# Two slots of 512 edges in each of two graph stages fetched row by row from SyncE's queue, in a two-network GNN kernel

## The reference, cut to what matters

```python
h = jnp.maximum(_layernorm(x), 0.0)
# first network, layers 0 and 1
msg = relu(x[src] + edge_attr)            # a gather of 100,000 rows of 512 bytes
agg = segment_sum(msg, dst, 6250)
h = (x + agg) @ W1 + b1; h = relu(batchnorm(h)); h = relu(h @ W2 + b2)
# second network, layers 2 and 3
agg = segment_sum(x[src], dst, 6250)
h = relu(((1 + eps) * x + agg) @ wA.T + bA) @ wB.T + bB
```

## Time and profile before

| | |
|---|---|
| median of 3 runs | 2780.12 us |
| the profiled execution | 2776.51 us |
| its span, first to last instruction | 2774.5 us |
| POOL busy | 1948.0 us (70%) |
| PE busy | 1915.5 us (69%) |
| DVE busy | 1712.8 us (62%) |
| ACT busy | 744.9 us (27%) |
| granted TensorE clock, mean | 0.846 of full |

### The profile page before, as it was taken

How to read it: one execution, slowest core, us unless ns; L and a number is a source line. 1 busy time by engine, 2 the same in 40 slices (tenths; PEclk the granted TensorE clock), 3 DMA queues, 4 the chain that set the end, 5 groups by cost and what they waited for, 6 DMA issues and landing times.

```text
span 2774.5 us, 30336 instructions
## 1 busy us (share of the span) xinstructions
PE 1915.5 (69%) x9233; PEld 1265.2 (46%) x9233; DVE 1712.8 (62%) x2755; ACT 744.9 (27%) x1002; POOL 1948.0 (70%) x2060
## 2 busy tenths in 40 slices
PE   3566565656665672656565666665678999989999
PEld 2444444434444442434343444433444565545656
DVE  7887777777776754777677767777764212442223
ACT  4222222222223241333333333333362000220001
POOL 6777777777777727777777777777706777367773
PEclk8788787777778886888778888888778999999999
DMA  6344333343434332444444444544425665466653
GB/s 198 113 128 120 113 112 115 116 125 113 128 112 143 120 116 85 121 149 128 142 135 150 134 151 148 162 152 157 142 83 193 222 211 199 140 205 214 219 191 115
DMA packets 224861, 403.74 MB, mean 146 GB/s; under 512 B 41224, under 2 KB 129116, under 8 KB 224740
## 3 DMA queue, kind: packets, MB, share of 16 engines
q1 hardware_dynamic: 159204, 267.94, 28.0%
q0 software_dynamic: 65536, 134.35, 18.3%
HBM read 337.92 MB, written 64.21 MB: 145 GB/s over the span
## 4 chain that ended last, share of the span: by engine, by line
POOL 47%; PE 26%; issue 17%; DVE 6%; DMA 3%; DVEq 1%; ACT 1%; POOLq 0%; SPq 0%; ACTq 0%
POOL xg L566 47%; PE psA L1354 17%; PE psG L1369 4%; DMA xg<-node_table,src_all 3%; PE psG L1418 2%; PE psA L1426 1%; DVE cell_room L960 1%; DVE xp_room L968 1%; DVEq L907 1%; DVE acc L885 0%; PE psG L1333 0%; PE psG L1448 0%; DVE xp_room L949 0%; DVE hid L932 0%; DVE hid L1065 0%
## 5 line engine op out<-in xcount | busy, mean ns | idle before, releaser
L566 POOL DMA_INDIRECT xg<-node_table,src_all x1536 | 1450.9, 945 | 513.5 <-issue 462.0
L1333 PE MATMUL psG<-hid,xp_room 128*128 128x160 f32 x3072 | 611.3, 374 | 414.0 <-DVE hid L932 400.8
L1333 PEld LDWEIGHTS psG<-hid,xp_room 128*128 128x128 f32 x3072 | 591.4, 253 | 466.1 <-issue 453.7
L1317 PE MATMUL psA<-cell_room,xp_room 128*128 128x512 f16 (+1 forms) x2176 | 552.4, 406 | 335.9 <-ACT count_out L633 247.8
L960 DVE TENSOR_SCALAR cell_room<-psG,cell_all 128x980 f16<-128x980 int16 x1088 | 712.2, 712 | 0.0
L586 POOL DMA_INDIRECT xg<-node_table,idx x480 | 461.2, 961 | 256.6 <-issue 253.2
L641 ACT COPY psG<-xp_room 128x512 f32<-128x512 f32 x384 | 226.4, 590 | 1246.7 <-DVE xp_room L968 1228.9
L968 DVE TENSOR_TENSOR xp_room<-psG,xg 128x512 f32<-128x512 f32 x384 | 261.9, 682 | 403.4 <-DMA xg<-node_table,src_all 399.0
L1317 PEld LDWEIGHTS psA<-cell_room,xp_room 128*128 128x128 f16 x2176 | 215.2, 104 | 629.8 <-ACT count_out L633 281.3
L885 DVE TENSOR_TENSOR acc<-acc,product 128x40 f32 x192 | 39.0, 203 | 395.3 <-ACT product L693 371.7
L932 DVE SCALAR_TENSOR_TENSOR hid<-loc_all,round_off,psG 128x2560 f32<-128x2560 f32 x96 | 274.7, 2861 | 0.0
(11 more groups left out here) (145 smaller groups left out, 794.3 us busy)
## 6 DMA issues: line engine op xcount, KB each, us to landing
xp_room<-in_edge_attr_dram SPq DMA_DIRECT2D x98, 768.0 KB, 4.8
cell_room<-count_store SPq DMA_DIRECT2D x16, 3000.0 KB
count_store<-count_out SPq DMA_DIRECT2D x96, 490.0 KB, 3.2
hid<-count_store SPq DMA_DIRECT2D x16, 2880.0 KB
xp_room<-in_edge_attr_dram SPq DMA_DIRECT2D x98, 256.0 KB, 5.1
xg<-node_table,src_all POOLq DMA_INDIRECT x1536, 2.5
node_table<-rows_h SPq DMA_DIRECT2D x48, 256.0 KB, 2.3
xg<-node_table,idx POOLq DMA_INDIRECT x480
```

The lines of the kernel that those rows point to most:

```text
L566: nc.gpsimd.indirect_dma_start(xg[:, n % 2, u, j, :], None, x if n < RAW_TURNS else table, bass.IndirectOffsetOnAxis(ap=src_all[:, s, j:j ...
L1317: last = nc.tensor.matmul(psA[:, bank, 0:w], src_hot[:, hots(n) % 2, i, :], cells[:, c % CELL_RING, c0:c0 + w], start=(c == first), stop=( ...
L1333: last = nc.tensor.matmul(psG[:, q, h * WIN:(h + 1) * WIN], ea[:, t, u, j, :], rows[:, u, j, :], start=(u == slots[0] and j == 0), stop=(u ...
```

## The change

In each of layers 0 and 1, slot 2 of turns 25 and 48 is no longer gathered by GpSimd. SyncE fetches its 512 rows with 512 DMAs of one row each. The address comes from a register: for each partition one load brings its four source numbers from `src_all` into registers, and four DMAs follow. They are handed out over the turns before: six partitions (24 DMAs) in each of turns 2 to 22 and two partitions in turn 23 for the slot of turn 25, and likewise in turns 26 to 46 and 47 for the slot of turn 48. They stand at the end of SP's turn, behind the attribute load. The rows go to a buffer of their own, `row_slot`, and `slot_sum` reads it for these slots.

```diff
+ROW_SLOT = 2
+ROW_TURNS = (25, TURNS - 1)
+ROW_STARTS = (2, 26)
+ROW_STEP = 6
...
+def by_rows(n, u):
+
+    return u == ROW_SLOT and n % TURNS in ROW_TURNS
+
+
+def landed(n, u):
+
+    return sum(not by_rows(t, u) for t in range(n % 2, n + 1, 2))
...
-        product = sb("product", [P, UPG, CW])
+        row_slot = sb("row_slot", [P, EPP * D])
+        product = row_slot[:, 0:UPG * CW].rearrange("p (s c) -> p s c", s=UPG)
...
+            def gather_rows(layer, t):
+
+                for k, (first, used) in enumerate(zip(ROW_STARTS, ROW_TURNS)):
+                    p0 = (t - first) * ROW_STEP
+                    if not 0 <= p0 < P:
+                        continue
+                    if t == first:
+                        sp.wait_ge(table_written, 16 * GROUPS * (layer + 1))
+                        if layer or k:
+                            last = (layer * TURNS + ROW_TURNS[k - 1] - (0 if k else TURNS)) * SLOTS + ROW_SLOT
+                            sp.wait_ge(summed, last + 1)
+                    s = used * SLOTS + ROW_SLOT
+                    for p in range(p0, min(p0 + ROW_STEP, P)):
+                        _, rows = nc.values_load_multi_w_load_instructions(
+                            src_all[p:p + 1, s, :], [mybir.EngineType.SP], min_val=0, max_val=NODES - 1,
+                            skip_runtime_bounds_check_because="the load checks its address against the table itself")
+                        for j, row in enumerate(rows):
+                            sp.dma_start(row_slot[p:p + 1, j * D:(j + 1) * D],
+                                         table[bass.DynSlice(row, 1), :]).then_inc(row_landed[k], 16)
...
                         load_turn(n + RING)
+                    gather_rows(layer, n % TURNS)
...
                     for u in range(SLOTS):
+                        if by_rows(n, u):
+                            continue
                         h = u // len(HALVES[0])
-                        if n >= 2 and u == HALVES[h][0]:
+                        if n >= 2 and u == min(v for v in HALVES[h] if not by_rows(n, v)):
...
                 dve.wait_ge(ea_staged, (n - RAW_TURNS) * SLOTS + u + 1)
-                dve.wait_ge(gathered[n % 2][u], 16 * EPP * (n // 2 + 1))
+                rows = xg[:, n % 2, u, :, :].rearrange("p j d -> p (j d)")
+                if by_rows(n, u):
+                    k, rows = ROW_TURNS.index(n % TURNS), row_slot[:, :]
+                    dve.wait_ge(row_landed[k], 16 * SUP * (n // TURNS + 1))
+                else:
+                    dve.wait_ge(gathered[n % 2][u], 16 * EPP * landed(n, u))
```

More of the change, by code:

```diff
@@ L345, in gnn_kernel @@
         gathered = [[sem(f"gathered{q}_{u}") for u in range(SLOTS)] for q in range(2)]
+        row_landed = [sem(f"row_landed{k}") for k in range(len(ROW_TURNS))]
         ea_staged = sem("ea_staged")
@@ L966, in slot_sum @@
                 dve.wait_ge(ea_staged, (n - RAW_TURNS) * SLOTS + u + 1)
-                dve.wait_ge(gathered[n % 2][u], 16 * EPP * (n // 2 + 1))
-                nc.vector.tensor_tensor(ea[:, n % RING, u, :, :].rearrange("p j d -> p (j d)"), ea_stage,
-                                        xg[:, n % 2, u, :, :].rearrange("p j d -> p (j d)"),
+                rows = xg[:, n % 2, u, :, :].rearrange("p j d -> p (j d)")
[4 more added lines that the diff above has]
+                    dve.wait_ge(gathered[n % 2][u], 16 * EPP * landed(n, u))
+                nc.vector.tensor_tensor(ea[:, n % RING, u, :, :].rearrange("p j d -> p (j d)"), ea_stage, rows,
                                         ALU.add).then_inc(summed, 1)
```

## The result

The changed kernel takes 2763.04 us in the median of four runs (2761.65 to 2765.65), the kernel before 2780.26 on the same chip (2774.67 to 2781.86, four runs). The ratio is 0.9942, with an interval of 0.9929 to 0.9954: faster, by 13 to 20 us. 2768 was forecast, and 2762 to 2773 as its own range. The profiled executions, 2761.72 and 2776.51 us, are 14.8 us apart, and the trace accounts for this difference. The gain of 11.6 us was given against the same execution. By the medians the gain is 17.2 us where 12 was forecast, so the result lies near the low end of the range.

The account below looks back on a forecast made before the run. GpSimd's issue of gathers was taken as the bound; 1.6 us from layer 0 and 10.0 from layer 1 sum to 11.6, about 12, giving 2768 us against the median. The range was 2757 to 2786, the forecast's own 2762 to 2773.

Parts of the forecast that it names:

- The bound: GpSimd's gathers in layers 0 and 1 set the pace, 1.249 us each; one not issued is worth 1.25 us.
- the new wait at the end of layer 0: DVE before slot 2 of turn 48: waits 7 us or more for rows issued in turn 47.
- the full gain of layer 1: End of layer 1: rows in time by some 0.6 us, so all 10.0 us are gained.
- SyncE's room in a turn: SyncE's steady turn: needs 16.4 to 16.7 us of 20, so it is in time every turn.
- one row DMA: Row fetch on SyncE: each DMA's issue takes 0.43 us, range 0.34 to 0.54.
- load of four registers: Row fetch on SyncE: one load per partition takes 0.8 us, range 0.3 to 1.28.
- gain of layer 0, at that sum: Slot 3's sum at layer 0's end: 996.6 instead of 998.24, a gain of 1.6 us, not 10.
- The landing of the last rows: End of layer 0: last two partitions issued until 992.8, landing taken as 2.5 us, so there at 995.3.
- Rival 3: Both layers: the full 20 us is gained, 2760, needing layer 0's last rows at 988; chance 0.06.
- Rival 2: Late stores delay ACT's evictions; layer 0's gain and part of layer 1's lost, 2773 to 2780; chance 0.17 with rival 4.
- Rival 4: 2048 small DMAs slow GpSimd's gathers, costing at most what the step gives; chance 0.17 together with rival 2.
- rival 1: SyncE becomes the bound above 3.1 us a partition: slower, about 2855 at 3.4 us; chance 0.17.

Follow-up runs that it names:

- the kernel one turn earlier: Against the changed kernel, turn 48's slot is fetched in turns 25 to 46, not 26 to 47: 2757.19 us, ratio 0.9908 to the kernel before.

## Why the prediction was right, and where it was not

The bound was right: each gather not issued gave 1.25 us (gathers still 1.249 us apart; the last of layer 0 issued 10.41 us earlier, of which 0.5 was there before turn 25). So were the new wait at the end of layer 0, the full gain of layer 1 with a gather as the last thing to arrive, and SyncE's room in a turn. By its steps:

| step | predicted | measured |
|---|---|---|
| one row DMA | 0.43 (0.34 to 0.54) | 0.228; 0.41 to 0.48 from one row's start to the next's, with two register instructions |
| load of four registers | 0.8 (0.3 to 1.28) | 0.562 in the median; 0.68 as 2.33 - 4 x 0.412 |
| one partition | 2.5 (1.7 to 3.4) | 2.33 |
| SyncE's turn, with attributes and one store | 16.4 | 15.3 |
| wait before slot 2 of turn 48, layer 0 | 7 to 11 | 7.76 |
| sum of slot 3, layer 0 | 996.6 | 993.92 |
| gain of layer 0, at that sum | 1.6 | 4.32 |
| gain of layer 1, at its last sum | 10.0 | 9.99 |
| last products of layer 1 | nothing | 1.94 |
| behind layer 1 | nothing | -1.46 |
| sum | 11.6 | 14.8 |

The one term of the sum that was mis-sized is layer 0's end, by 2.7 us, and it has two parts. The landing of the last rows was put at 2.5 us from the rows for stores and gathers; it is 1.14 us from the end of the last issue (991.43) to the sum (992.57), and 1.68 at the end of layer 1 (2003.74 to 2005.42). That is 1.36. The other 1.2 is the start: turn 47's products were over, and SyncE free, at 985.58 instead of 986.8. They began at 979.58, 0.4 later than 5.0 us ahead of before, but took 5.97 us in place of 7.59. The prediction moved the row of 7.59 rigidly by 5.0 us and did not ask whether its length would stay. The windows over these products, before and changed, show what set the length (the granted clock stands third from the end):

```profile
984.20:991.80 7.60, 7.59 (x34) 7.60 (x35) 4.52 (x5) 2.17 (x3) 5.66 (x6) 0.60 0.31 78
979.58:985.55 5.97, 5.97 (x32) 5.73 (x32) 4.53 (x5) 1.29 (x3) 4.45 (x6) 0.76 0.42 133
```

Length times granted clock is 4.55 and 4.54 us, and 4.55 (6.60 at 0.69) in the kernel one turn earlier: the same work at another clock. It doesn't follow the wait just ahead of them, which was 6.77 us before and 7.54 in the changed kernel, so this part, 1.2 us of the gain, is luck as far as the prediction goes. From the first attribute load to the end of the eight rows were 5.85 us, 6.0 predicted.

The 1.94 us of layer 1's last products and the 1.46 us lost behind layer 1 had no place in the sum; that they nearly cancel is luck too. TensorE's clock after an idle stretch was a price that the rows of before already held: at the end of layer 1 the first sixteen products of turn 48 took 2.41 us there, right behind other products, and the last sixteen 4.38.

Rival 3 (the full 20 us) named the right condition, that the last rows be there at 988; the kernel with an earlier start meets it, and gains 25.7 us by medians and 19.6 by its profiled execution. Rival 2 did not happen: ACT's wait for stores isn't among the long waits of the changed kernel. Rival 4 is refuted by the kernel in which nobody fetches, whose gathers go through layer 1 at the same rate (967.41 against 967.50 us). For rival 1, the point of 3.1 us a partition is consistent with six and with ten partitions a turn, and its size at the end (44 us for 21 turns of 2.1) is of the kind that was measured (202 for 48 of about 4.5). The prediction looked for it in the price of a DMA; what brought it on with six partitions a turn was a condition in which SyncE's instructions come one in 0.70 us. Nothing in the trace of before shows that condition, and the forecast holds only outside of it: inside it the sign is the other one, by 10%.

The Trainium skill's rule in "DMA: Bandwidth & Descriptors", "Rules for kernel authors" (join many small transfers) was named beside rival 1. No run joins the transfers, so the rule itself wasn't tried; what the experiments show is that it didn't decide here: 2048 transfers of 512 bytes cost nothing measurable in one condition, and 36 us in the other. The 0.6 us that the prediction gave beside its own 0.8 for a load of registers is near the measured median of 0.562, but it is no floor: the shortest load took 0.313.

What stays open: what causes the disturbed condition, and why skipped gathers give 20 us in it; where the 1.5 us behind layer 1 go; what sets the granted clock of turn 47's products, since the wait ahead of them doesn't order it; and whether the meeting of the last gather with the attribute load can be kept away on purpose, since no kernel was made for it.

## What to carry to other kernels

Work that is moved to an idle queue is priced by how it fits the period of that queue's other duties, and by when its last piece is issued: six small units in each turn were free, ten in each cost 7%, and two units in the last turn cost 5 us that an edit of one number gave back. When a term is moved earlier, look at its length again too: the last sixteen products of layer 1 took 2.44 us instead of 4.38 behind a shorter wait, and turn 47's products of layer 0 5.97 instead of 7.59 at a higher granted clock. And count the instructions that are added to a turn, not their bytes alone: 6656 on one engine were free in one condition and cost 397 us in another, so a gain of half a per cent is not the whole account of this change.

## What the runs showed of the hardware that was not expected

- A DMA of one row of 512 bytes with its address in a register took SyncE 0.228 us for the instruction and 0.41 to 0.48 from start to start, and its row was in use 1.1 to 1.7 us after the last one's issue ended.
- A load of four values into registers took 0.562 us in the median (0.313 to 1.263).
- A gather of 128 rows landed 2.5 us after its issue in the median, but 4.3 to 5.7 us when a 768 KB load was issued between 1.5 us ahead of it and 0.5 us behind (27 gathers in three traces).
- Sixteen products of the same shape took 4.25 to 4.38 us after TensorE had stood 5.4 to 6.8 us, 3.90 after 4.34, 3.72 after 3.98, and 2.44 after 1.6 or less. Thirty-two took 7.59, 6.60, 6.26 and 5.97 us at granted clocks of 0.60, 0.69, 0.73 and 0.76.
- A program was seen in two conditions, on the same chip at different times: 2.78 and 3.69 ms for the kernel before. In the longer one instructions of several engines begin in stretches one in 0.70 us, while a gather and the packets that bring instructions keep their lengths.
